# Feed forward of a decoder layer: the mean's subtraction and two dequantizing scales on POOL, and DVE's maximum over the gelu values ahead of the input's

## What is computed

```python
def _layer_norm(x):
    mu = jnp.mean(x, axis=-1, keepdims=True)
    xc = x - mu
    var = jnp.mean(xc * xc, axis=-1, keepdims=True)
    return xc * jax.lax.rsqrt(var + EPS_LN)

def _activation_quant(x):
    scale = 127.0 / jnp.clip(jnp.max(jnp.abs(x), axis=-1, keepdims=True), EPS_ACT)
    return jnp.clip(jnp.round(x * scale), -128, 127) / scale

def _bitlinear(x, w, b):
    xn = _layer_norm(x)
    xq = _activation_quant(xn)
    wq = _weight_quant(w)
    return jnp.einsum('bsd,fd->bsf', xq, wq) + b
h = _bitlinear(x, w1, b1)          # 512 -> 2048
h = jax.nn.gelu(h, approximate=False)
return _bitlinear(h, w2, b2)       # 2048 -> 512
```

## Time and profile before

| | |
|---|---|
| time, median of 3 runs | 890.78 us (887.35 to 894.88) |
| profiled execution: its own time | 888.06 us |
| profiled execution: span of the instructions | 886.3 us |
| feed forward's steps 4 to 15 (first output L2310 at 754.76, thirteenth at 860.14) | 105.38 us, 8.78 each |
| busy in the whole span | PE 92%, DVE 84%, ACT 57%, POOL 16% |

### The profile page before, as it was taken

One profiled execution on the slowest core, in us unless ns is written; L12 is line 12 of the kernel. 1 busy time (PEld: TensorE's weight loads), 2 busy tenths in 40 slices (PEclk: granted clock), 3 DMA queues, 4 the chain that ended last, 5 costly groups with the idle time before them and its releaser, 6 DMA issues.

```text
span 886.3 us, 23348 instructions
## 1 busy us (share of the span) xinstructions
PE 811.3 (92%) x9881; PEld 649.0 (73%) x9898; DVE 743.9 (84%) x1206; ACT 507.0 (57%) x727; POOL 139.0 (16%) x197
## 2 busy tenths in 40 slices
PE   3677999999999999998989899999999978999996
PEld 2665988888888888888877788888888845444442
DVE  5898889889897988988486589889888989999994
ACT  4555374654637465461733354535435457999994
POOL 1001010110201011010102000000000123676431
PEclk9998999999999999999999999999999999999999
DMA  8311103030120302015050422430331230243221
GB/s 241 131 51 70 50 14 109 14 87 24 48 74 14 108 15 72 16 48 193 2 192 1 143 87 82 144 120 22 142 142 67 68 97 25 92 135 114 90 79 40
DMA packets 36406, 72.31 MB, mean 82 GB/s; under 512 B 6064, under 2 KB 6832, under 8 KB 35288
## 3 DMA queue, kind: packets, MB, share of 16 engines
q1 hardware_dynamic: 35768, 68.86, 23.7%
q0 software_dynamic: 544, 2.10, 0.7%
HBM read 58.33 MB, written 12.58 MB: 80 GB/s over the span
## 4 chain that ended last, share of the span: by engine, by line
PE 70%; DVE 15%; issue 6%; POOL 4%; ACT 4%; DMA 0%; DVEq 0%; ACTq 0%; POOLq 0%
PE P L62 11%; PE P L64 9%; PE P L63 9%; PE S L711 5%; PE S L2215 5%; PE P L2203 4%; POOL sm L373 3%; DVE E L1802 3%; PE P L797 2%; DVE xf L965 2%; PE S L62 2%; PE S L63 2%; PE S L64 2%; PE S L1663 2%; PE P L635 2%
## 5 line engine op out<-in xcount | busy, mean ns | idle before, releaser
L373 POOL TENSOR_TENSOR sm<-sm,mhalf 128x16 f32<-128x16 f32 x8 | 30.6, 3829 | 311.9 <-DVE sm L1060 311.9
L2215 PE MATMUL S<-wq,hqT 128*128 128x512 bf16 x255 | 59.9, 380 | 4.2 <-ACT hqT L2146 4.2
L711 PE MATMUL S<-R,K 64*64 64x32 f32 x3072 | 57.7, 222 | 3.9 <-issue 2.0
L711 PEld LDWEIGHTS S<-R,K 64*64 64x64 f32 x3072 | 51.6, 136 | 10.9 <-issue 6.3
L2203 PE MATMUL P<-wq,xqT 128*128 128x512 bf16 x240 | 55.8, 386 | 2.5 <-ACT xqT L2132 1.7
L965 DVE TENSOR_TENSOR xf<-P,xx 128x1024 f32<-128x1024 f32 x40 | 48.8, 1221 | 10.2 <-PE P L635 10.2
L1802 DVE TENSOR_SCALAR E<-S,upper 128x2048 f32<-128x2048 f32 x16 | 37.6, 2349 | 23.2 <-PE S L1650 23.0
L1476 ACT ACTIVATE E<-E 128x2048 f32<-128x2048 f32 x16 | 30.6, 1914 | 45.8 <-DVE E L1802 45.8
L1808 DVE RECIPROCAL rec<-S 128x512 f32<-128x512 f32 x16 | 53.6, 3350 | 0.3 <-PE S L1665 0.3
L972 DVE TENSOR_TENSOR xf<-xf,xnT 128x1024 f32<-128x1024 f32 x40 | 49.1, 1227 | 1.1
L1008 DVE TENSOR_TENSOR R<-R,D 128x256 f32<-128x256 f32 x96 | 40.4, 421 | 8.8 <-PE S L711 8.8
(11 more groups left out here) (291 smaller groups left out, 2664.9 us busy)
## 6 DMA issues: line engine op xcount, KB each, us to landing
wch<-in_wff SPq DMA_DIRECT2D x32, 256.0 KB, 3.2
cwch<-in_wff SPq DMA_DIRECT2D x8, 1024.0 KB, 6.9
xt<-in_x SPq DMA_DIRECT2D x8, 512.0 KB, 4.5
y<-in_x SPq DMA_DIRECT2D x8, 512.0 KB, 3.6
out<-y SPq DMA_DIRECT2D x8, 512.0 KB, 3.2
cxt<-out SPq DMA_DIRECT2D x8, 512.0 KB, 4.4
ct<-in_ctx SPq DMA_DIRECT2D x8, 512.0 KB, 5.2
cxr<-out SPq DMA_DIRECT2D x8, 512.0 KB, 6.8
```

The lines of the kernel that those rows point to most:

```text
L373: pool.tensor_tensor(sm[:, 2, :], sm[:, 1, :], mhalf[:, 0:2 * H], ALU.pow).then_inc(y_rstd, 1)
L711: mm = pe.matmul(ps[half_rows(side), par, b, k, :], K[head_rows(par), r % 2, at:at + HALF], right_tokens(par, g, side, i), start=True, sto ...
L2215: mm = pe.matmul(O[:, :], hqT[b % 2][:, k, :], w2q[:, k, :], start=k == 0, stop=k == NF - 1)
```

## The change

Four moves, all within the feed forward:

1. x minus its mean (L2248 on DVE) becomes POOL's, a tensor_scalar at the head of its `front(f)`, behind a wait for the mean. The mean's tile `mv` is doubled, and DVE's bn_aggr waits for POOL's subtraction of two steps earlier.
2. The input's dequantizing scale (L2268 on DVE) becomes POOL's, a new function `scale_x(f)` called behind `front(f)`, so behind the six instructions of the pieces and ahead of `middle(m)`.
3. The gelu values' dequantizing scale (L2296 on DVE) becomes POOL's, at the end of `middle(m)`, behind a wait for the clip.
4. DVE's order in a step: `front` without the maximum, `middle(m)` (maximum over the gelu values), `front_most(f)` (the maximum over x), `middle_variance(m)`, then `front_inverse(f)`, which stood ahead of `middle(m)`, `front_scale(f)`, `middle_scale(m)`.

```diff
@@ gpsimd
         def front(f):
+            x = xt[f % 2]
+            pool.wait_ge(s_aggr, f + 1)
+            pool.tensor_scalar(x[:, :], x[:, :], mv[f % 2][:, 0:1], None, ALU.subtract).then_inc(s_xc, 1)
             pool.wait_ge(s_var, f + 1)
...
+        def scale_x(f):
+            pool.wait_ge(s_xclip, f + 1)
+            if f >= 2:
+                pool.wait_ge(s_gelu, f - 1)
...
+            pool.tensor_tensor(s1[f % 2][:, 4:5], s1[f % 2][:, 2:3], ws127[:, 0:1], ALU.mult).then_inc(s_xdq, 1)
+
         def middle(m):
             pool.wait_ge(s_var2, m + 1)
...
+            pool.wait_ge(s_hclip, m + 1)
+            pool.tensor_tensor(s2[m % 2][:, 9:10], s2[m % 2][:, 6:7], ws127[:, 1:2], ALU.mult).then_inc(s_hdq, 1)
 
         def step(f, t, m, b, o):
             if f is not None:
                 front(f)
+                scale_x(f)
             if m is not None:
                 middle(m)
@@ vector
-            dve.bn_aggr(mv[:, :], st[:, :]).then_inc(s_aggr, 1)
+            if f >= 2:
+                dve.wait_ge(s_xc, f - 1)
+            dve.bn_aggr(mv[f % 2][:, :], st[:, :]).then_inc(s_aggr, 1)
...
-            dve.tensor_scalar(x[:, :], x[:, :], mv[:, 0:1], None, ALU.subtract).then_inc(s_xc, 1)
+
+        def front_most(f):
...
             dve.wait_ge(s_xc, f + 1)
             dve.tensor_reduce(s[:, 2:3], x[:, :], AX_X, ALU.max, apply_absolute_value=True).then_inc(s_xmax, 1)
@@ def front_scale
-            if f >= 2:
-                dve.wait_ge(s_gelu, f - 1)
...
-            dve.tensor_scalar(s[:, 4:5], s[:, 2:3], ws127[:, 0:1], None, ALU.mult).then_inc(s_xdq, 1)
@@ def middle_scale
-            dve.tensor_scalar(s[:, 9:10], s[:, 6:7], ws127[:, 1:2], None, ALU.mult).then_inc(s_hdq, 1)
@@ def step
                 front(f)
-                front_inverse(f)
             if m is not None:
                 middle(m)
+            if f is not None:
+                front_most(f)
+            if m is not None:
                 middle_variance(m)
             if f is not None:
+                front_inverse(f)
                 front_scale(f)
             if m is not None:
                 middle_scale(m)
```

More of the change, by code:

```diff
@@ L1986, in ffn_parts @@
     st = sb("fst", [P, 6])
-    mv = sb("fmv", [P, 2])
+    mv = [sb(f"fmv{n}", [P, 2]) for n in range(2)]
     s1 = [sb(f"s1_{n}", [P, 8]) for n in range(2)]
@@ L2083, in front @@
                     pool.tensor_tensor(pr[:, i + 1:i + 2], pr[:, i:i + 1], pc[:, 3 * i:3 * i + 1], ALU.subtract).then_inc(s_pres, 1)
+        def scale_x(f):
+            pool.wait_ge(s_xclip, f + 1)
+            if f >= 2:
+                pool.wait_ge(s_gelu, f - 1)
+            if f == 0:
+                pool.wait_ge(s_unit, 2)
+            pool.tensor_tensor(s1[f % 2][:, 4:5], s1[f % 2][:, 2:3], ws127[:, 0:1], ALU.mult).then_inc(s_xdq, 1)
         def middle(m):
@@ L2118, in rest, with front_whole @@
                 step(*turns(n))
-        return {"open": open_early, "front": front, "middle": middle, "step": lambda n: step(*turns(n)), "rest": rest}
+        def front_whole(f):
+            front(f)
+            scale_x(f)
+        return {"open": open_early, "front": front_whole, "middle": middle, "step": lambda n: step(*turns(n)), "rest": rest}
     def scalar(act):
@@ L2244, in front @@
             dve.memset(fspare[:, :], 0.0)
-            dve.bn_aggr(mv[:, :], st[:, :]).then_inc(s_aggr, 1)
+            if f >= 2:
+                dve.wait_ge(s_xc, f - 1)
+            dve.bn_aggr(mv[f % 2][:, :], st[:, :]).then_inc(s_aggr, 1)
             dve.wait_ge(s_aggr, f + 1)
-            dve.tensor_scalar(s[:, 1:2], mv[:, 1:2], 1.0 + EPS_LN, EPS_LN * EPS_LN, ALU.mult, ALU.add).then_inc(s_var, 1)
-            dve.tensor_scalar(x[:, :], x[:, :], mv[:, 0:1], None, ALU.subtract).then_inc(s_xc, 1)
+            dve.tensor_scalar(s[:, 1:2], mv[f % 2][:, 1:2], 1.0 + EPS_LN, EPS_LN * EPS_LN, ALU.mult, ALU.add).then_inc(s_var, 1)
+        def front_most(f):
+            x, s = xt[f % 2], s1[f % 2]
             dve.wait_ge(s_xc, f + 1)
@@ L2263, in front_scale @@
             x, s = xt[f % 2], s1[f % 2]
-            if f >= 2:
-                dve.wait_ge(s_gelu, f - 1)
-            if f == 0:
-                dve.wait_ge(s_unit, 2)
-            dve.tensor_scalar(s[:, 4:5], s[:, 2:3], ws127[:, 0:1], None, ALU.mult).then_inc(s_xdq, 1)
             dve.wait_ge(s_xrec, f + 1)
```

## The result

The changed kernel takes 913.94 us (median of 5 runs, 910.98 to 917.14), the kernel before 892.04 us (5 runs, 887.35 to 894.88). The ratio is 1.024 (1.0206 to 1.0273). The profiled execution took 917.14 us, its span 915.3. The prediction was 906.0 us with a range of 900 to 912: the direction and the mechanism are right, the time lies just outside the range.

The account below looks back on a forecast made before the run. DVE's gapless 8.62 us chain bounds the kernel, PE and ACT close behind. Steps 4 to 15 +15.4, step 3 +1.06, batch 2 +0.3: together +16.8, 904.9 profiled or 907.6 median; it said 906, range 900 to 912.

Parts of the forecast that it names:

- the 1.91 from the reciprocal to the power: Steps 4 to 15, POOL: gelu values' power starts 1.91 us after DVE's reciprocal, behind pieces and input's scale; bounds 1.8 to 2.1.
- the price of the subtraction for batch 2: Front of batch 2, standing alone: DVE waits for POOL's subtraction, taken as 0.8 us against 0.51, so +0.3 us.
- The relief of DVE: DVE's chain of 8.62 us per step loses the subtraction and two small instructions: 0.5 to 0.6 us if nothing else moved.
- busy time over 10 us lower: Sign that the forecast is right: DVE's busy time falls by over 10 us.
- The new wait: Full steps: late reciprocal delays POOL's pieces and power; DVE idles 1.3 to 1.5 us ahead of the gelu values' clip.
- From the power to gm's end 2.86: Each full step: 2.86 us from POOL's power to the end of DVE's gm, which xb runs into.
- The second limit by ACT's squares: From step 5: variance needs ACT's squares, 5.02 us after gm's end, making the loop 10.10 us; step 4 takes 9.68.
- The cover of the subtraction: Full steps: POOL's subtraction hides under the 2.19 us gelu maximum, with 0.3 us left behind an extra instruction; cost nothing.
- Drain and fronts of batches 0 and 1 at zero: Steps 16 to 19 have no front and cost 0; batch 1 has 0.56 us idle behind it and costs nothing.
- A: Rival: the gain comes through, loop 8.5 us, 884 to 887 us, if reciprocal to power is under 0.9; chance 0.04.
- B: Rival: squares' limit does not bind, all twelve steps take 9.68 us, 900 profiled, 903 median; chance 0.07.
- C: Rival: code load paid at POOL's first subtraction, batch 0 ends 6 us late, 4 us added, 909 to 912; chance 0.07.

Follow-up runs that it names:

- the second profile: Both kernels, unchanged, run and profiled once more: 895.21 us for the kernel before, 911.67 us for the changed kernel.

## Why the prediction was 8 us off, and right in its mechanism

The 8 us first: the forecast's +16.8 was 5.1 short of the 21.9 between the medians, the median of the kernel before moved by 1.3 with two more runs (890.78 to 892.04), and the prediction said 906 where its own sum gave 907.6, 1.6 more. The step that failed is the 1.91 from the reciprocal to the power; the price of the subtraction for batch 2 comes second. Point by point, by its own steps:

- **The relief of DVE**, 0.5 to 0.6 a step: 6.7 us less busy in twelve steps. The number is right partly by luck: the three instructions that left had more, since the subtraction took 0.77 in six of the steps beside a 1024-wide instruction of POOL, and gm, now 1.59 instead of 1.44, took 1.6 back. It is worth nothing, as said. The sign "busy time over 10 us lower" didn't come, in the whole span it is 8.3 (743.9 to 735.6), and didn't follow from 0.5 to 0.6 a step.
- **The new wait**: POOL's power behind the pieces and the scale, DVE's clip behind the power. Right, 1.7 us a step where 1.3 to 1.5 were forecast. The order alone gives 16.8 us.
- **From the power to gm's end 2.86**: 844.70 + 1.59 - 843.42 = 2.87. Right, and the variants with the residual addition early show that 0.30 of it is xb's hold on gm.
- **The second limit by ACT's squares**: DVE waits 0.3 to 0.5 for them. Right: with the reciprocal ahead of the variance, 0.5 a step comes back. At step 4 it doesn't bind, as predicted: 9.78 against the 9.68 of the working.
- **From the reciprocal to the power 1.91, bounds 1.8 to 2.1**: the step that failed in the loop. It is 1.91 in four of twelve steps, but 2.15 or 2.16 in seven and 2.40 in one, and in the second profile 2.15 or more in all. The number was put together from lengths that POOL's instructions had while DVE ran a reduction beside them; moved behind the reciprocal, the first cast falls beside DVE's fxm. Twelve steps: 122.59 (123.61 in the second profile) against 120.8, so 1.8 to 2.8 us.
- **The fronts without cover, +0.3 for batch 2**: +1.08 (4.43 from its bn_aggr to the next batch's, against 3.35). The price was at fault: POOL's subtraction takes 1.57 us, outside the bounds of 0.48 to 1.25 from the nearest rows. That a one-input instruction can't be longer than a two-input one of the same width was an assumption without a row. Step 3 became 1.31 longer instead of 1.06, the 0.25 of the longer cast.
- **The cover of the subtraction**: it was to be ready 0.3 ahead of DVE behind a 1024-wide instruction. It isn't: it ends at 829.56 in such a step, and DVE's maximum over x starts at 829.60, 2.36 behind the maximum over the gelu values instead of 2.19. The 0.17 costs nothing, since DVE then waits 0.33 for the squares instead of 0.51.
- **Drain and fronts of batches 0 and 1 at zero**: right for batches 0 and 1. But the first stretch has the 1.34 us that no wait explains, and the drain is 1.94 longer: 0.25 in step 16, which takes 8.58 instead of 8.33 (8.35 in the second profile of before), and 1.68 in its last 16 matmuls. The second profile of before has 0.52 of the 1.34 and all of the 1.68 by itself: the profile on which the sum was built had caught PE at full clock in both places. This is a term the sum did not have.

These terms are 1.8 (loop), 0.8 (batch 2), 0.2 to 0.3 (step 3), 0.25 (step 16) and 3.0 (clock), together 6.1: with the sum's 16.8 they make the 22.9 us by which the feed forwards of the two first profiles differ. The second profiles, both with the lower clock at the end, are 21.7 apart, close to the 21.9 of the medians, and there the 4.9 us that are missing are 2.8 (loop), 1.0 (batch 2 and step 3), 0.2 (step 16) and 0.8 (clock behind the first bn_aggr). So more than half of what the sum lacked is the loop's.

The rivals: A fell (with the power first the wait is gone, and the kernel isn't faster). Its turning point, 0.9 from reciprocal to power, fits only a gm of 1.29; with the sum's own 2.86 it is 8.78 - 5.02 - 0.31 - 2.86 = 0.6. B fell, since the squares do bind. C fell: the subtraction of batch 0 starts as soon as bn_aggr is done and takes 1.57 like the others, without a gap of 6 us:

```profile
718.77 1.57 POOL L2067 TENSOR_SCALAR fxt<-fxt,fmv 128x512 f32<-128x512 f32 x1 [9.50 <-DVE fmv L2265]
```

What the prediction had missed of rival A is the second branch. Its argument against A was POOL's queue; the experiment that mends the queue shows that A fails for a second reason, PE's transposes of the pieces. Anyone who had mended the order by the prediction's words would have won nothing here.

No version beat the kernel before. The nearest is the one with the scales alone, which is no different from it. That PE and ACT are busy for 104 and 103 of the 105 us of steps 4 to 15 in the kernel before doesn't make this the floor, since their busy time shrinks with the step. The scales with the early residual show it in their last five of the twelve steps:

```profile
826.37:868.97 42.60, 42.34 (x284) 20.93 (x287) 39.35 (x85) 42.30 (x46) 20.16 (x55) 1.00 0.27 87
```

These are 8.52 us each, where the kernel before takes 8.65. In them PE and ACT are 99% busy. A version that keeps these steps and gm's guard in the other six was not run.

## What to carry to other kernels

Before moving work to an idle engine, look where in its in-order list the result that others wait for can start, and follow every consumer of that result: here the late reciprocal had two, and freeing one moved the bound to the other. The durations of POOL's small instructions held here only beside the DVE instructions they were measured beside, so in a new order check which large DVE instruction each falls next to. And a seemingly wasteful place in a list (the residual addition ahead of gm) may be what keeps a longer instruction away from the critical one.

## What the hardware showed unexpectedly

- DVE's full-width products with a scalar operand (gm, fxm, the subtraction) and POOL's instructions run one after the other, for the whole of the one that came first, both ways. POOL first: gm takes 1.29 alone, 1.59 behind xb, 3.17 behind a 1024-wide one. DVE first: a 128x1 instruction of POOL takes 1.26 instead of 0.19 behind gm, a cast 0.50 instead of 0.21 behind fxm. DVE's reductions aren't affected: the maximum over the gelu values is 2.27 or 2.28 with POOL's subtraction beside it or not. The Trainium skill (SBUF — State Buffer, "SBUF: two separate sides") calls the port pair that POOL shares with DVE an exclusive lock, which a POOL instruction and a DVE instruction in a 2-port mode, or with two inputs in SBUF, hold for the whole instruction, whichever starts first. The trace agrees by these numbers; no row shows the mode in which gm and fxm run.
- A race too close to be seen in the printed starts decides between a step of 10.08 and one of 10.33, and falls otherwise in another execution of the same kernel.
- POOL's subtraction of a per-row scalar from 128x512 takes 1.57 us, the same with the scalar as a repeated second operand 1.04, and an addition of two full tensors 1.27. The Trainium skill (GPSIMD Engine Reference, "Performance versus the Vector engine") gives 769 ns as the best case for 512 elements and sets the two-input instruction apart as the costlier one per element. The scalar form here takes twice as long as that best case and is the slowest of the three. By the page the term for batch 2 was +0.3, by the trace it is +1.08.
- The same 16 matmuls at the end take 3.63 or 5.31 us from one execution of the same kernel to the next, by the granted clock. A single profile can't tell this from an effect of the change; here a second one of each kernel did.
